# When the second-to-last batch's outputs are taken: behind its value product, between the last score units

## The chip, the cores and the metric

One core of one Trainium2 chip runs the whole kernel. TensorE (PE in the profile, PEld for its weight loads), VectorE (DVE), ScalarE (ACT) and GpSimd (POOL) each run their own list of instructions in order and wait for one another by semaphores; SyncE (SP) issues most of the DMAs. The metric is the device time of one execution in microseconds. A change within 0.2% (1.6 us here) counts as no change.

## The reference, cut to what matters

Input is x of 16 batches x 256 rows x 256 columns, float32. Two layers, each `x = x + s * silu(ffn(xn))` with `xn = layernorm(x)`. In the first layer `s` is a diagonal linear recurrence; in the second, the one that this change touches, it is an attention with 16 heads and a compressed key and value:

```python
q = (x @ Wq).reshape(B, S, 16, 192)              # 128 plain, 64 rotated
kv = x @ Wkv_a                                   # 64 latent columns, 64 rotated keys
c_kv = rmsnorm(kv[..., :64]) * kv_norm_w
k_nope, v = split(c_kv @ Wkv_b)                  # 16 heads x (128 + 128)
scores = einsum('bqhd,bkhd->bhqk', q, k) / sqrt(192)
attn = softmax(where(causal, scores, min))
out = einsum('bhqk,bkhd->bqhd', attn, v).reshape(B, S, 2048) @ Wo
x = x + out * silu(ffn2(xn))                     # ffn2: base + gated low-rank experts
```

The kernel folds `Wkv_b`'s key half into the queries and its value half into `Wo`. So the attention works on the 64 latent columns: scores are query x (latent, rotated key), the value product gives 64 latent columns per head, and one product with a folded matrix (`woe`, 1024 x 256) gives the output.

## The kernel before, in words

The second layer runs batch by batch (16 batches, numbered 0 to 15) in one long software pipeline. A step `n` of the loop is one unit of scores, 10 units per batch, and every engine's program is the same loop over `n` with its own work for each step. The names in this document:

- `scores n` (`l1_s`, L773 for units of the kinds W and M, L766 for kind T): TensorE's product for unit n into one of two banks. It waits (`mx`) until VectorE has read the unit two before it.
- `read n` (`most`, L1608, with L1600 for kind T): VectorE adds the mask, takes the row minimum and writes the tile to SBUF.
- `exps n` (L1065, ScalarE), `inverse n` (L1615, VectorE), `normalise n` (L2051, GpSimd), `turn n` (`turn_weights`, L1631 and L1644, VectorE: the weights transposed into `PT`). On every engine read n stands in step n, exps n in step n+1, inverse and normalise n in step n+2, turn n in step n+4.
- `value product` (`l1_pv`, L795, TensorE), which needs the turned weights of its batch. Batch 14 takes it in one piece. Batch 15 takes it in two: the first piece (key blocks for the first 6 units, 150 to 155) and the last piece, which needs turn 159 and, since it writes into the same banks, the low parts of the first piece's query tile (`otl`).
- `latents` (L1078, ScalarE) copies the value product of one query tile (two instructions, 128x512 each) out of PSUM as the high parts `oh`; `low parts` (L1653, VectorE, two instructions) writes the rest, `ol`. There is one pair `oh`/`ol` for each of the two query tiles.
- `output` (`l1_out`, L549, TensorE): 8 blocks x 3 matmuls (high x low, low x high, high x high, helper `three`) of 128x256. Then `gated_out` (L1664, VectorE) multiplies with the gate, `residual` (L2113, GpSimd) adds x, and SyncE stores 128 rows of the result.

I write output 14a, 14b, 15a, 15b for the two query tiles of the last two batches, and likewise for latents and low parts. The last batch (units 150 to 159) takes its units in an order of its own: M, M, M, T, T, M, and then four of kind W.

What sets the order around the change is a table written out by hand. For batches 0 to 13 a fixed lag behind the batch's last unit says at which step its value product (V), latents and low parts (L), outputs (O), gated outputs (R) and residuals (C) come. For batches 14 and 15 the table `LAST` names the step directly, one pair of numbers (query tile a, tile b) per batch. `due(what, n, qt)` looks the step up, and all engines' loops and the list that deals out the six PSUM banks shared by these products (`shared_bank_order`) use it. Within one step the order on each engine is fixed: on TensorE value product, scores, output; on ScalarE latents, then exps n-1; on VectorE low parts, gated_out, inverse n-2, turn n-4, read n.

Of the kernel before, what the change touches and what calls it, by code (L numbers as in the profile page):

```python
# [141 lines left out]
def shared_bank_order():  # L142
# [34 lines left out]

LAST = {
    "V": ((154, 154), (160, 162)),
    "L": ((158, 159), (163, 166)),  # L180
    "O": ((159, 161), (165, 167)),
    "R": ((161, 165), (166, 171)),
    "C": ((164, 165), (168, 173)),
}
LAG = {"V": (LAG_V, LAG_V), "L": (LAG_L, LAG_L), "O": LAG_O, "R": LAG_R, "C": LAG_C}
STEPS = max(LAST["C"][1]) + 1
# [2071 lines left out]
```

How the kernel before makes its waits and increments, by code:

```python
    def wait_ge(self, name, value):  # L99
        if value > self.reached.get(name, 0):
            self.e.wait_ge(self.sems[name], value)
            self.reached[name] = value
# [287 lines left out]
        def after_weights(w):  # L390
            w.wait_ge("wo_t", 4)
            w.wait_ge("wml", 1)
            w.wait_ge("wmh", 1)
# [1 line left out]
        def after_first(w):  # L395
            w.wait_ge("wo_t", 2)
# [1 line left out]
        def after_up(w):  # L398
            w.wait_ge("f1", 8 * NC)
# [1 line left out]
        def after_mlp(w):  # L401
            w.wait_ge("f1", 8 * NC)
            w.wait_ge("f2", 16 * NC)
            w.wait_ge("hsl", 8 * NC)
            w.wait_ge("hsh", 8 * NC)
            w.wait_ge("bu", NC)
# [1 line left out]
        def after_l0(w):  # L408
            after_mlp(w)
            w.wait_ge("xo", 2 * NC)
            w.wait_ge("th0", 2 * NC)
            w.wait_ge("dx", 2 * NC)
            w.wait_ge("ty", 2)
# [1 line left out]
        def qt_free(w, n):  # L415
            if n == 0:
                after_up(w)
            elif n < 3:
                after_mlp(w)
            else:
                w.wait_ge("s", UNITS * ((n - 3) // 2) + HALF_DONE[(n - 3) % 2])
# [10 lines left out]
        def place(e, w, b, h, heads=range(4)):  # L433
            n = 2 * b + h
            w.wait_ge("qq", g_nth[2 * n + 1])
            qt_free(w, n)
            for i in heads:
                for j in range(2):
# [7 lines left out]
        @block.sync  # L447
# [26 lines left out]
                load_x(c)  # L474
            w.wait_ge("w1h", 4)
            w.wait_ge("w1l", 4)
# [22 lines left out]
            def spread(b):  # L500
                w.wait_ge("kvw", b + 1)
                if b == 0:
                    after_mlp(w)
```

## Time and profile before

| what | value |
|---|---|
| median of 3 runs | 791.5 us (791.44 to 791.93) |
| the profiled execution, its own time | 791.67 us |
| its span, first to last instruction | 789.9 us |
| PE, DVE, ACT, POOL busy | 778.6, 681.7, 524.5, 479.5 us |
| mean granted TensorE clock | 0.999 |

The profiled execution is 0.17 us over the median, and 1.8 us of its time lie around the span. TensorE counts as busy 99% of the span, since each matmul's record overlaps the next one's. Only in the last 30 us are there stretches in which it waits.

### The profile page before, as it was taken

What the parts mean: (1) busy time and instruction counts of PE and PEld (TensorE: products, weight loads), DVE (VectorE), ACT (ScalarE), POOL (GpSimd) and SP (SyncE); (2) the same over time, 40 slices, a digit from 0 to 9 for tenths busy, and PEclk for the clock granted to TensorE, in tenths of its full rate; (3) what the DMA queues carried; (4) which work ended last, traced back from release to release, by engine and by line L of the source; (5) the groups of instructions that cost most, each with busy time, mean ns of one, the idle gap of its engine ahead of it and who ended that gap; (6) DMA issues with size and microseconds to landing.
All of it is one profiled execution on the core that took longest, in us unless ns stands there. A gap on an engine that the chain in (4) does not pass through costs nothing.

```text
span 789.9 us, 23152 instructions
## 1 busy us (share of the span) xinstructions
PE 778.6 (99%) x7976; PEld 711.5 (90%) x7976; DVE 681.7 (86%) x2616; ACT 524.5 (66%) x1612; POOL 479.5 (61%) x1278
## 2 busy tenths in 40 slices
PE   9999999999999999999999999999999999999988
PEld 7889889888889889898998989899898998989867
DVE  6998897888688899989898998989989898998885
ACT  5554454445555787777767777677777867777682
POOL 6880202202236696776867768686776867768673
PEclk9999999999999999999999999999999999999999
DMA  8600220000002222322222322223222222322220
GB/s 302 253 2 2 62 82 27 1 1 1 1 15 52 40 46 52 61 54 36 48 46 50 64 39 50 40 46 55 56 55 35 48 46 49 63 39 53 34 52 28
DMA packets 101334, 41.15 MB, mean 52 GB/s; under 512 B 91744, under 2 KB 98400, under 8 KB 100576
## 3 DMA queue, kind: packets, MB, share of 16 engines
q1 hardware_dynamic: 98896, 38.89, 22.1%
q8 instruction: 63, 1.03, 0.5%
q10 hardware_dynamic: 2320, 0.79, 0.4%
q14 instruction: 55, 0.45, 0.2%
HBM read 14.47 MB, written 4.19 MB: 24 GB/s over the span
## 4 chain that ended last, share of the span: by engine, by line
PE 92%; DVE 4%; ACT 1%; POOL 1%; issue 1%; ACTq 0%; POOLq 0%; DVEq 0%
PE bank L549 63%; PE bank L773 11%; PE bank L795 8%; PE bank L766 3%; PE bank L629 2%; PE bank L815 1%; PE bank L566 1%; DVE SM L1608 1%; PE bank L681 1%; ACT SM L1065 1%; DVE PT L1631 1%; PE bank L641 1%; PE bank L655 1%; POOL SM L2051 1%; PE bank L700 0%
## 5 line engine op out<-in xcount | busy, mean ns | idle before, releaser
L1065 ACT ACTIVATE SM<-SM,stb 128x224 f32<-128x224 f32 (+7 forms) x512 | 207.2, 407 | 62.7 <-DVE stb L1608 58.2
L2051 POOL TENSOR_SCALAR SM<-SM,stb 128x224 f32<-128x224 f32 (+7 forms) x512 | 195.2, 396 | 67.5 <-DVE stb L1615 66.1
L549 PE MATMUL bank<-yh,wq_lo 128*128 128x256 f32 x512 | 150.6, 294 | 0.0
L549 PE MATMUL bank<-yh,wq_hi 128*128 128x256 f32 x512 | 144.7, 283 | 0.0
L549 PE MATMUL bank<-yl,wq_hi 128*128 128x256 f32 x512 | 144.6, 282 | 0.0
L773 PE MATMUL bank<-KT,QT 128*128 128x192 f32 (+4 forms) x640 | 120.9, 327 | 1.7 <-DVE stb L1608 1.7
L1608 DVE CUSTOM_DVE_ANT_0 SM<-bank,CONST 128x224 f32<-128x224 f32 (+3 forms) x320 | 97.2, 348 | 23.3 <-PE bank L773 20.9
L1631 DVE STREAM_TRANSPOSE PT<-SM 128x128 f32<-128x128 f32 (+2 forms) x232 | 99.7, 462 | 16.7 <-PE bank L795 16.7
L773 PEld LDWEIGHTS bank<-KT,QT 128*128 128x128 f32 x640 | 97.5, 190 | 5.3 <-DVE stb L1608 3.6
L549 PEld LDWEIGHTS bank<-yh,wq_lo 128*128 128x128 f32 x512 | 97.1, 190 | 1.4
L549 PEld LDWEIGHTS bank<-yh,wq_hi 128*128 128x128 f32 x512 | 97.1, 190 | 0.0
L549 PEld LDWEIGHTS bank<-yl,wq_hi 128*128 128x128 f32 x512 | 97.0, 189 | 0.0
L1065 ACT ACTIVATION_READ_ACCUMULATOR SM<-SM,stb 128x1 f32 x512 | 96.9, 189 | 0.0
L950 ACT ACTIVATE hs<-bank,B 128x512 f32<-128x512 f32 x64 | 44.0, 688 | 75.3 <-PE bank L549 70.2
L2044 POOL TENSOR_TENSOR QA<-QA 128x256 f32<-128x256 f32 x62 | 45.9, 740 | 58.7 <-DVE QA L1579 58.7
L1037 ACT ACTIVATE QT<-bank 64x512 f32<-64x512 f32 x128 | 75.6, 590 | 6.5 <-PE bank L549 5.0
L1579 DVE TENSOR_TENSOR QA<-bank,TR 128x512 f32<-128x512 f32 x124 | 79.4, 683 | 0.1
L549 PE MATMUL bank<-woe_hi,ol 128*128 128x256 f32 x256 | 75.4, 294 | 0.7 <-issue 0.7
L549 PE MATMUL bank<-w2h,hl 128*128 128x256 f32 x256 | 74.0, 289 | 0.2 <-DVE w2l L1352 0.2
L549 PE MATMUL bank<-w2h,hh 128*128 128x256 f32 x256 | 72.4, 283 | 0.0
L549 PE MATMUL bank<-w2l,hh 128*128 128x256 f32 x256 | 72.3, 283 | 0.0
L549 PE MATMUL bank<-woe_hi,oh 128*128 128x256 f32 x256 | 72.1, 281 | 0.0
(229 smaller groups left out, 2068.9 us busy)
## 6 DMA issues: line engine op xcount, KB each, us to landing
QT<-QA SPq DMA_DIRECT2D x240, 64.0 KB, 2.1
PT<-KV SPq DMA_DIRECT2D x256, 16.0 KB, 1.8
out<-fo SPq DMA_DIRECT2D x32, 128.0 KB, 2.0
X<-in_x SPq DMA_DIRECT2D x7, 512.0 KB, 11.5
stage<-in_wqn SPq DMA_DIRECT2D x2, 1024.0 KB, 5.3
stage<-in_wo SPq DMA_DIRECT2D x2, 1024.0 KB, 4.9
stage<-in_w1t SPq DMA_DIRECT2D x4, 256.0 KB, 5.0
stage<-in_w2t SPq DMA_DIRECT2D x2, 512.0 KB, 6.2
```

Source lines behind the costliest of these rows:

```text
L549: i = e.matmul(dst, a, b, start=(first and j == 0), stop=(last and j == 2), skip_group_check=skip)
L766: j = e.matmul(sbank[n % 2][32 * i:32 * i + 32, at:to], KT[b % 3][:, p, 32 * kb:32 * kb + 32], Q[:, :, kb:3, i, :], start=True, stop=True)
L773: j = e.matmul(sbank[n % 2][:, at], Q[:, q, :, :].rearrange("p h c -> p (h c)"), KT[b % 3][:, p, 0:32 * q + 32], start=True, stop=True)
L795: j = e.matmul(sums[64 * half:64 * half + 64, :, 32 * q:32 * end], C[rows_, kb // 2, at], PT[rows_, 2 * half:2 * half + 2, kb, q:end, :], ...
L950: e.activation(hs[g % 2][:, :], fbank[g % 2][:, :], ACT.Gelu, bias=B1[:, g % 8:g % 8 + 1]).then_inc(SEM["gelu"], 1)
L1037: i = e.activation(QT[r, (2 * b + g // 2) % 3, p, :, g % 2:4:2, :].rearrange("p n j c -> p j n c"), src[r, :, :, :], ACT.Copy)
L1065: i = e.activation(M[:, at], M[:, at], ACT.Exp, bias=S[:, 0, j:j + 1], scale=-1.0, accum_out=S[:, 1, j:j + 1])
L1579: i = e.tensor_tensor(A[:, part, :, :, g % 2, :], src, TR[:, part, :].rearrange("p (n c) -> p n c", n=8).unsqueeze(1).broadcast_to([128, 2 ...
L1608: i = e.tensor_tensor_reduce(M[:, at], bk[:, at], mask[:, 224 - 32 * q:256], 1.0, 3e38, ALU.add, ALU.min, S[:, 0, j:j + 1])
L1631: return e.transpose(PT[:, slot, 0:k, q:q + some, :].rearrange("p k q c -> p q k c"), src)
L2044: e.tensor_tensor(A[:, 0, 0, :, :], A[:, 0, 0, :, :], A[:, 1, 1, :, :], ALU.subtract)
L2051: i = e.tensor_scalar(P[:, at], P[:, at], S[:, 2, j:j + 1], 1.0, ALU.mult, ALU.mult)
```

## The change

Five rows of the table `LAST` are there; four of them change. Batch 14's latents, low parts, outputs, gated outputs and residuals move to other steps, and batch 15's first latents and low parts move from step 163 to step 164. No instruction is added or removed, none changes its form.

```diff
 LAST = {
     "V": ((154, 154), (160, 162)),
-    "L": ((158, 159), (163, 166)),
-    "O": ((159, 161), (165, 167)),
-    "R": ((161, 165), (166, 171)),
-    "C": ((164, 165), (168, 173)),
+    "L": ((155, 157), (164, 166)),
+    "O": ((156, 158), (165, 167)),
+    "R": ((160, 165), (166, 171)),
+    "C": ((163, 166), (168, 173)),
 }
```

On TensorE, from scores 155 (three matmuls) on. A group of L549 is one output of 24 matmuls; here only its first row stands. The first L773 pair is scores 156. Before:

```order
L773 MATMUL bank<-KT0,QT 128x224 [waits mx]
L773 MATMUL bank<-KT0,QT 128x256
...
L549 MATMUL bank<-woe_hi,ol0 128x256 [waits z1,otl,oth]
...
L795 MATMUL bank<-PT 64x2x192 [waits otl,oth,c1,pt]
...
L549 MATMUL bank<-woe_hi,ol1 128x256 [waits ob]
...
L795 MATMUL bank<-PT 64x2x64 [waits otl,pt]
```

And now:

```order
L773 MATMUL bank<-KT0,QT 128x224 [waits mx]
L773 MATMUL bank<-KT0,QT 128x256
L549 MATMUL bank<-woe_hi,ol0 128x256 [waits z1,otl,oth]
...
L549 MATMUL bank<-woe_hi,ol1 128x256 [waits otl,oth]
...
L773 MATMUL bank<-KT0,QT 128x224 [waits mx]
L773 MATMUL bank<-KT0,QT 128x256
L795 MATMUL bank<-PT 64x2x192 [waits c1,pt]
...
L795 MATMUL bank<-PT 64x2x64 [waits otl,pt]
```

Before, scores 156 to 159 stood together, output 14a behind them and output 14b between the two pieces of batch 15's value product. Now output 14a stands behind scores 156, output 14b behind scores 158, and nothing is left between scores 159, the first piece and the last piece.

On VectorE, the end of its list, from read 159's last instruction on. L1653 is low parts 15a, the last L1631 of each piece is turn 159, L1664 is the gated output. Before:

```order
L1615 RECIPROCAL stb2<-stb2 128x2 [waits p]
L1631 STREAM_TRANSPOSE PT<-SM1 128x2x8x32 [waits n]
L1664 SCALAR_TENSOR_TENSOR fo0<-bank,PT 128x256 [waits out0,o]
L1615 RECIPROCAL stb3<-stb3 128x2 [waits p]
L1631 STREAM_TRANSPOSE PT<-SM2 128x2x8x32 [waits n]
L1631 STREAM_TRANSPOSE PT<-SM3 128x2x8x32 [waits n]
L1653 TENSOR_TENSOR ol0<-bank,oh0 128x512 [waits oth,pv]
L1653 TENSOR_TENSOR ol0<-bank,oh0 128x512 [waits oth]
L1631 STREAM_TRANSPOSE PT<-SM4 128x2x8x32 [waits n]
```

And now:

```order
L1664 SCALAR_TENSOR_TENSOR fo0<-bank,PT 128x256 [waits out0,o]
L1615 RECIPROCAL stb2<-stb2 128x2 [waits p]
L1631 STREAM_TRANSPOSE PT<-SM1 128x2x8x32 [waits n]
L1615 RECIPROCAL stb3<-stb3 128x2 [waits p]
L1631 STREAM_TRANSPOSE PT<-SM2 128x2x8x32 [waits n]
L1631 STREAM_TRANSPOSE PT<-SM3 128x2x8x32 [waits n]
L1631 STREAM_TRANSPOSE PT<-SM4 128x2x8x32 [waits n]
L1653 TENSOR_TENSOR ol0<-bank,oh0 128x512 [waits oth,pv]
L1653 TENSOR_TENSOR ol0<-bank,oh0 128x512 [waits oth]
```

Low parts 15a and turn 159 have changed places, and gated output 14a stands one step earlier. Earlier in the same list low parts 14a now stand ahead of inverse 153 (before: of inverse 156), and low parts 14b ahead of inverse 155 (before: of inverse 157). On ScalarE latents 14a now stand between exps 153 and exps 154, latents 14b between exps 155 and exps 156. GpSimd's and SyncE's lists are the same as before. In the deal of the banks, output 15a now takes the bank of output 14a and output 15b that of output 14b.

## Rows read from the trace of the kernel before

**Rows 1.** Chain of waits in order of time: start us, length us, what
```profile
748.46 0.81 PE bank L773 x4
...
772.14 0.77 DVE PT L1631 x2
...
772.96 2.60 PE bank L795 x92
775.56 3.04 PE bank L549 x24
...
780.52 3.05 PE bank L549 x24
```

**Rows 2.** Timeline of TensorE: start, length, instruction, idle before
```profile
748.29 0.97 PE L773 MATMUL bank<-KT,QT 128*128 128x224 f32 x4
...
758.44 4.22 PE L795 MATMUL bank<-PT 32*64 32x512 f32 x128
...
765.13 1.08 PE L773 MATMUL bank<-KT,QT 128*128 128x224 f32 x4 [0.65 <-DVE stb L1608]
...
769.76 0.36 PE L549 MATMUL bank<-woe_hi,ol 128*128 128x256 f32 x1 [0.71 <-issue]
...
772.56 0.28 PE L549 MATMUL bank<-woe_hi,oh 128*128 128x256 f32 x1
...
778.53 1.99 PE L795 MATMUL bank<-PT 32*64 32x128 f32 x128
```

**Rows 3.** Timeline of VectorE, same columns
```profile
749.30 0.39 DVE L1608 CUSTOM_DVE_ANT_0 SM<-bank,CONST 128x224 f32<-128x224 f32 x1 [0.24 <-PE bank L773]
...
763.57 0.14 DVE L1615 RECIPROCAL stb<-stb 128x6 f32<-128x6 f32 x1
...
765.13 0.19 DVE L1615 RECIPROCAL stb<-stb 128x6 f32<-128x6 f32 x1
...
768.37 1.29 DVE L1653 TENSOR_TENSOR ol<-bank,oh 128x512 fp32r<-128x512 f32 x2 [0.46 <-ACT oh L1078]
769.57 0.16 DVE L1615 RECIPROCAL stb<-stb 128x2 f32<-128x2 f32 x1
...
770.87 1.29 DVE L1653 TENSOR_TENSOR ol<-bank,oh 128x512 fp32r<-128x512 f32 x2
...
772.82 0.36 DVE L1608 CUSTOM_DVE_ANT_0 SM<-bank,CONST 128x224 f32<-128x224 f32 x1
...
774.68 0.17 DVE L1615 RECIPROCAL stb<-stb 128x2 f32<-128x2 f32 x1
774.76 1.28 DVE L1631 STREAM_TRANSPOSE PT<-SM 128x512 f32<-128x512 f32 x2
776.31 1.29 DVE L1653 TENSOR_TENSOR ol<-bank,oh 128x512 fp32r<-128x512 f32 x2 [0.27 <-ACT oh L1078]
777.52 0.70 DVE L1631 STREAM_TRANSPOSE PT<-SM 128x512 f32<-128x512 f32 x1
```

**Rows 4.** Timeline of ScalarE, same columns
```profile
762.99 0.32 ACT L1065 ACTIVATE SM<-SM,stb 128x32 f32<-128x32 f32 x1 [0.38 <-DVE stb L1608]
...
765.11 0.41 ACT L1065 ACTIVATE SM<-SM,stb 128x128 f32<-128x128 f32 x1
...
766.27 0.19 ACT L1065 ACTIVATION_READ_ACCUMULATOR SM<-SM,stb 128x1 f32 x1
...
767.74 1.09 ACT L1078 ACTIVATE oh<-bank 128x512 fp32r<-128x512 f32 x2
...
775.61 1.09 ACT L1078 ACTIVATE oh<-bank 128x512 fp32r<-128x512 f32 x2 [0.96 <-PE bank L795]
```

**Rows 5.** Timeline of GpSimd: normalise 159
```profile
774.94 0.91 POOL L2051 TENSOR_SCALAR SM<-SM,stb 128x224 f32<-128x224 f32 x2 [0.32 <-DVE stb L1615]
```

**Rows 6.** Busy times by stretch; behind POOL the granted clock, DMA share
```profile
786.00:787.00 1.00, 0.41 (x4) 0.20 (x2) 0.42 (x1) 0.00 (x0) 0.05 (x1) 1.00 0.11 35
...
788.50:789.00 0.50, 0.00 (x0) 0.00 (x0) 0.00 (x0) 0.00 (x0) 0.00 (x0) 0.94 0.77 260
```

## The prediction

> **What bounds the kernel now.** The edit touches only the last 30 us, so I went first to the chain of waits there, in order of time, then to the timelines of the engines it passes through. In the chain [rows 1] VectorE's turn 155 ends at 772.91, and it releases the first piece of batch 15's value product at 772.96. From there TensorE never waits: first piece 2.60, output 14b 3.04, last piece (starts 778.53 [rows 2]), output 15a 3.05, output 15b. So two things set the end: when VectorE has done its list up to turn 155, and how much TensorE work stands behind that point.
>
> Before 772.96 TensorE does wait. In its timeline [rows 2] scores 157 start at 765.13 after 0.65 us of waiting for read 155, and output 14a starts at 769.76 after 0.71 us. VectorE is the engine that nearly all of this waits for: in its timeline [rows 3] the marked gaps are 0.46 at 768.37 (low parts 14a, waiting for ScalarE's latents) and 0.27 at 776.31. The change moves an output of 24 matmuls from behind 772.96 to before it. The question is whether TensorE's own sum was the bound behind 772.96, or only just covered something else.
>
> **The change, step by step.** I replay the stretch with the durations of before. TensorE's value product of batch 14 starts at 758.44 and lasts 4.22 [rows 2]. All up to there is untouched.
>
> Latents 14a. ScalarE took latents 15a 0.05 behind the value product (first piece 772.96 + 2.60 [rows 1], latents 775.61 [rows 4]), so latents 14a start at 762.71. They last 1.09 and now stand ahead of exps 154, which started at 762.99 and now start at 763.80: 0.81 later. Inverse 154, which came 2.14 behind that start (765.13 [rows 3]), can go from 765.94. VectorE is itself later than that by now, so this costs nothing.
>
> Low parts 14a. On VectorE they now stand ahead of inverse 153 (763.57 [rows 3]). Their first input is ready at 762.71 + 0.63 (latents 767.74 [rows 4] to low parts 768.37 [rows 3]) = 763.34. The pair takes 1.20 to the next instruction (768.37 to 769.57 [rows 3]). So all that follows is 1.20 later: read 155 ends and exps 155 start at 765.11 + 1.20 = 766.31.
>
> Output 14a. It can start 1.39 behind its low parts (768.37 to 769.76 [rows 2, 3]): 764.96, and takes 2.92 (24 matmuls, the last starts at 772.56 [rows 2], 0.12 apart). TensorE is free at 767.88, then takes scores 157 and 158 at 0.81 each (the chain's row of 748.46 [rows 1]): 769.50. Scores 157 are up to 2.75 later than before, but VectorE comes to read them only some 0.7 behind 769.5 (below), so it does not notice.
>
> Latents and low parts 14b. ScalarE does exps 155 from 766.31 for 1.35 (765.11 to 766.27 + 0.19 [rows 4]), then latents 14b at 767.68, low parts 14b at 768.31. That is where low parts 14a were before (768.37), and VectorE again waits for ScalarE there, some 0.6 us: the 0.46 of before, one unit less in front of it (1.30, from 769.57 to 770.87 [rows 3]), one pair of low parts more (1.20), rounded. VectorE goes on at 769.51.
>
> Output 14b. 768.31 + 1.39 = 769.70, done at 772.62. It stands ahead of scores 159. So scores 159 start at 772.62, and VectorE can read them 1.01 later (748.29 [rows 2] to 749.30 [rows 3]): 773.63, not 772.82 as before. VectorE would be there at 769.51 + 2 units at 1.30 + 0.75 (turn 155, from 770.87 + 1.20 to 772.82) = 772.86, and waits 0.77. This wait is new.
>
> First piece. Turn 155 is done in time, so it starts behind scores 159 at 772.62 + 0.81 = 773.43: 0.47 later than before. It ends at 776.03.
>
> The tail. Before, inverse 159 came 1.86 behind the start of read 159 (772.82 to 774.68 [rows 3]); now 773.63 + 1.86 = 775.49. The gated output 14a, moved ahead of it, lies in the wait for exps 159 as it did before. Then turns 157, 158, 159 at 0.64 each (two took 1.28 [rows 3]) from 775.57: turn 159 ends at 777.49. GpSimd's normalise 159 is done 1.17 behind inverse 159 (774.94 + 0.91 [rows 5], against 774.68), at 776.66, in time for turn 159 at 776.85. Latents 15a start at 776.08 and give their first half at 776.71, also in time. Low parts 15a start at 777.50, and the last piece, which needs them, 1.39 later: 778.89. Before it started at 778.53 [rows 2]. Behind it nothing changes: the last piece, outputs 15a and 15b, gate, residual, store.
>
> So output 14b's 3.04 us do leave the tail, and in their place TensorE waits 776.03 to 778.89 = 2.86 us, for a chain on VectorE that output 14b had hidden. The sum is +0.36 us.
>
> Things that I cost at nothing: the bank deal (output 15a now waits for gated output 14a, done by 774.7; output 15b for gated output 14b, which VectorE does behind low parts 15a, near 779.1, over four us before it is wanted); the residuals and stores of batch 14, which GpSimd and SyncE do while idle. If gated output 14b were late by its own length of about 0.4 nothing would follow.
>
> **Bounds.** From below: suppose VectorE waits nowhere from 763.57 on. It was done with turn 159 at 777.52 + 0.62 = 778.14 with low parts 15a in front of it [rows 3], the same work as now, and had waited 0.46 + 0.27 + some 0.2 of small gaps. So it could be done at 777.2 and the last piece start at 777.4: -1.1 us. From above: each step that I hid may cost its own size. The two waits on VectorE (0.6 and 0.77) could each grow by half a microsecond, giving about +1.4. I take the replay, +0.36.
>
> The profiled execution took 791.67 us, so the sum is 792.03; it lies 0.17 over the median of 791.5, so the forecast is 791.9 as a median.
>
> **Rivals.** A, the forecast: TensorE's saved cover comes back as a wait, 791.9, within about 790.9 to 793.0.
>
> B, better packing: the two VectorE waits shrink since latents 14b or scores 159 come earlier than I have them. For it: TensorE's own waits before 772.96 add up to over 1.3 us in two rows alone [rows 2], and the freed output fills them. Against it: the order on each engine is fixed, and both waits follow from an instruction that stands in front (exps 155, output 14b). At its bound it is -1.1 us, about 790.4; its middle is 791.0. It cannot reach 789.9, which is 0.2% under the median, so it too is mostly "no change". 0.2% is 1.6 us, about what can be told from no change here.
>
> C, slower: the clock falls in the new gap. At the very end of the trace TensorE's last matmul ends at 786.41 and the granted clock, 1.00 at first, averages 0.94 from 788.50 to 789.00 [rows 6]: it fell from 2.4 to 1.2 GHz at about 788.94, some 2.5 us after the last matmul. The new wait of 2.86 us is longer than that. For it: that row. Against it: no inner wait of this trace is near this length, none shows a fall, and one fall in one execution does not say that each such wait brings one. If the clock falls before 778.89, the 48 matmuls of the last two outputs, 0.12 apart, run at the lower level for as long as it lasts. If all of them take twice their time that is +5.7 us, with the last piece's 1.99 up to +7.7; if it is up again after one output, +2.9. No row shows how soon it rises. I take +2.9 on top of the 0.36: 794.8. It decides from a wait of 2.5 us up; with a VectorE chain 0.4 shorter it is gone.
>
> The Trainium skill, TensorE: Matmul & The Clock Gate, section Part 1: The HAM clock gate, says that the clock is at half rate by default, that activity releases it, and that the check runs on its own time, not the kernel's. By that rule this stretch would come out slower in some executions and not in others. The trace agrees as far as the fall at 788.94 goes; the recovery no row here shows. From the same page (Back-to-back issue gap), 256 columns take 213 ns cold; by that the 48 matmuls would cost an estimated +4.5 us if all ran cold, not +5.7.
>
> D, the change does nothing: were the last piece bound by something that did not move, the time would be 791.5. Nothing in the trace has that place; the number is inside A.
>
> **Chances.** A (with D) 0.72, B 0.13, C 0.15. Slower by over 0.2% (above 793.1): nearly all of C and a little of A, 0.15. Faster by over 0.2%: 0.04, since B's bound stops short of it. Same: 0.81. The forecast is A's, 791.9. The range reaches down to B's bound, 790.5, and up through A's +1.4 into C's mild cases, 793.8; about 0.1 is left out above and little below.
>
> **What the profile will show.** Right: outputs 14a and 14b on TensorE near 765.0 and 769.7; VectorE idle for about 0.8 us before read 159, released by TensorE's scores 159; the chain of waits going through VectorE's turns and low parts 15a into the last piece, with TensorE idle from 776.0 to 778.9; the granted clock at 1.00 throughout. Wrong: a first piece that starts before 773.0 or after 774.2; output 14b waiting past 770.5; low parts 15a waiting for ScalarE rather than for turn 159; a clock under 1.00 between 776 and 786, which would be C. A time under 789.9 would break the bound on VectorE's work, and so the whole replay.

## The result, and the profile after

The changed kernel takes 793.21 us (median of 22 executions, 791.53 to 794.35), the kernel before 791.53 us (median of 22, 791.34 to 792.82). The means have a ratio of 1.0016, with a 95% interval of 1.0010 to 1.0023; the medians are 1.68 us or 0.21% apart. So the change is slower, but the interval reaches to both sides of the 0.2% that I had named as the limit, and whether it is slower by more than that stays open. The time lies in my range (790.5 to 793.8), but 1.3 us above the forecast, and the likeliest case was not the one that happened. Rival C was.

The profiled execution took 793.82 us, its span is 792.0 us, against 791.67 and 789.9. The chain of waits of after, in order of time, has these pieces at its end (start us, length us, what):

```profile
765.35 3.09 PE bank L549 x24
768.43 1.62 PE bank L773 x8
770.05 3.07 PE bank L549 x24
773.12 0.82 PE bank L773 x4
...
776.01 1.16 DVE PT L1631 x2
...
777.73 1.26 DVE ol L1653 x2
...
779.12 2.51 PE bank L795 x118
781.63 4.07 PE bank L549 x24
```

The order is the one foreseen. Output 14a (765.35), scores 157 and 158, output 14b (770.05), scores 159 stand in a row. Then the chain leaves TensorE for VectorE's turns and low parts 15a (777.73) and comes back with the last piece. Of before's chain [rows 1], output 14b (775.56) is gone from between the pieces. What is new are two lengths: the last piece takes 2.51 instead of 1.99 [rows 2], output 15a 4.07 instead of 3.05.

TensorE's timeline of after around that place (start, length, instruction, idle before):

```profile
758.87 4.21 PE L795 MATMUL bank<-PT 32*64 32x512 f32 x128
```

```profile
779.12 2.51 PE L795 MATMUL bank<-PT 32*64 32x128 f32 x128 [2.66 <-DVE ol L1653]
781.56 0.58 PE L549 MATMUL bank<-woe_hi,ol 128*128 128x256 f32 x1
...
783.01 0.41 PE L549 MATMUL bank<-woe_hi,ol 128*128 128x256 f32 x1
783.22 0.41 PE L549 MATMUL bank<-woe_lo,oh 128*128 128x256 f32 x1
...
784.32 0.28 PE L549 MATMUL bank<-woe_hi,oh 128*128 128x256 f32 x1
784.44 0.28 PE L549 MATMUL bank<-woe_hi,ol 128*128 128x256 f32 x1
```

The same place in the trace of before, where output 15a starts at full speed:

```profile
780.45 0.39 PE L549 MATMUL bank<-woe_hi,ol 128*128 128x256 f32 x1
```

And the stretches of after (from:to, its length, busy time and instructions of PE, PEld, DVE, ACT, POOL; then the granted clock, DMA share, GB/s):

```profile
776.00:778.00 2.00, 0.46 (x40) 0.32 (x21) 2.00 (x5) 1.09 (x2) 1.71 (x4) 1.00 0.03 8
778.00:779.00 1.00, 0.00 (x0) 0.00 (x0) 1.00 (x3) 0.00 (x0) 0.00 (x0) 1.00 0.38 129
779.00:780.00 1.00, 0.88 (x61) 0.91 (x66) 0.30 (x1) 0.00 (x0) 0.61 (x1) 1.00 0.01 2
780.00:781.00 1.00, 1.00 (x71) 1.00 (x63) 0.00 (x0) 0.00 (x0) 0.11 (x1) 0.70 0.02 7
781.00:782.00 1.00, 1.00 (x32) 0.88 (x19) 0.00 (x0) 0.33 (x1) 0.00 (x0) 0.50 0.42 140
782.00:783.00 1.00, 1.00 (x6) 1.00 (x6) 0.63 (x2) 0.76 (x2) 0.00 (x0) 0.50 0.00 0
783.00:784.00 1.00, 1.00 (x7) 1.00 (x7) 0.66 (x2) 0.00 (x0) 0.00 (x0) 0.60 0.00 0
784.00:785.00 1.00, 1.00 (x11) 1.00 (x10) 0.00 (x0) 0.00 (x0) 0.00 (x0) 1.00 0.00 0
```

TensorE waits 2.66 us ahead of the last piece, for low parts 15a. At about 780.4 the granted clock falls from 2.4 to 1.2 GHz (its mean is 0.70 from 780 to 781, 0.50 from there) and is back at about 783.8 (0.60 from 783 to 784). In between output 15a's matmuls start 0.21 apart, afterwards 0.12, as everywhere before. TensorE works all through the low stretch: it waits first, and pays later.

The difference of the two profiled executions, 2.1 us of span, comes out in three parts:

- 0.43 us stand there before the instructions of the two kernels differ: batch 14's value product starts at 758.87, not at 758.44 [rows 2].
- From that start to the last piece it is 779.12 - 758.87 = 20.25 us, before 778.53 - 758.44 = 20.09 [rows 2]. The new order costs 0.16.
- From the last piece's start to output 15b it is 781.63 + 4.07 - 779.12 = 6.58 us, before 780.52 + 3.05 - 778.53 = 5.04 [rows 1, 2]. The low clock costs 1.54.

0.16 + 1.54 = 1.70, and the medians are 1.68 apart. That these agree so closely is in part chance, since executions differ by more than that, but the clock splits them: 16 of the 22 have a mean granted clock of 0.997 or 0.998 and took 793.12 us or more (793.56 on average), the other 6 have 1.0 and took 791.53 to 792.70 (792.18 on average).

The 0.43 us arise long before the first instruction that differs. From one value product near 290 us to the next near 325 it is 33.93 us in before (290.64 to 324.57) and 34.74 in after (290.27 to 325.01), so a lead of 0.37 turns into a lag of 0.44. In between TensorE waits 0.58 us, at 306.73, for a product of VectorE (L1579) that had itself waited for a DMA; the trace of before has neither wait. VectorE's timeline of after:

```profile
305.30 1.29 DVE L1579 TENSOR_TENSOR QA<-bank,TR 128x512 f32<-128x512 f32 x2 [1.88 <-DMA QT<-QA]
```

### The profile page after: what moved, and what is told of

It is laid out like the page before. It is cut to its first block, busy times and chain, and to the rows that moved or that the text cites. A ratio compares the mean times of both kernels' runs of the same rounds, so it can differ in the third digit from the quotient of the medians.

```text
span 792.0 us, 23152 instructions
## 1 busy us (share of the span) xinstructions
PE 779.1 (98%) x7976; PEld 712.3 (90%) x7976; DVE 681.2 (86%) x2616; ACT 522.7 (66%) x1612; POOL 480.3 (61%) x1278
## 4 chain that ended last, share of the span: by engine, by line
PE 90%; SPq 4%; DVE 2%; issue 1%; DMA 1%; ACT 1%; POOL 0%; POOLq 0%; DVEq 0%
PE bank L549 63%; PE bank L773 12%; PE bank L795 8%; SPq L512 3%; PE bank L766 2%; PE bank L629 2%; SPq L441 1%; PE bank L566 1%; PE bank L681 1%; PE bank L641 1%; PE bank L655 1%; DMA QT<-QA 0%; PE bank L700 0%; ACT SM L1065 0%; PE bank L706 0%
## 5 line engine op out<-in xcount | busy, mean ns | idle before, releaser
L549 PE MATMUL bank<-yh,wq_lo 128*128 128x256 f32 x512 | 150.5, 294 | 0.0
L549 PE MATMUL bank<-yh,wq_hi 128*128 128x256 f32 x512 | 144.6, 282 | 0.0
L549 PE MATMUL bank<-yl,wq_hi 128*128 128x256 f32 x512 | 144.6, 282 | 0.0
L773 PE MATMUL bank<-KT,QT 128*128 128x192 f32 (+4 forms) x640 | 120.4, 327 | 0.4 <-DVE stb L1608 0.4
L1631 DVE STREAM_TRANSPOSE PT<-SM 128x128 f32<-128x128 f32 (+2 forms) x232 | 99.3, 459 | 16.0 <-PE bank L795 16.0
L773 PEld LDWEIGHTS bank<-KT,QT 128*128 128x128 f32 x640 | 97.6, 190 | 2.8 <-DVE stb L1608 1.1
L549 PEld LDWEIGHTS bank<-yh,wq_lo 128*128 128x128 f32 x512 | 97.1, 190 | 1.4
L549 PEld LDWEIGHTS bank<-yh,wq_hi 128*128 128x128 f32 x512 | 97.0, 190 | 0.0
L549 PEld LDWEIGHTS bank<-yl,wq_hi 128*128 128x128 f32 x512 | 97.0, 189 | 0.0
L1579 DVE TENSOR_TENSOR QA<-bank,TR 128x512 f32<-128x512 f32 x124 | 79.3, 682 | 2.0 <-DMA QT<-QA 1.9
L549 PE MATMUL bank<-woe_hi,ol 128*128 128x256 f32 x256 | 75.9, 297 | 0.4 <-issue 0.4
L549 PE MATMUL bank<-w2h,hl 128*128 128x256 f32 x256 | 74.0, 289 | 0.2 <-DVE w2l L1352 0.2
L549 PE MATMUL bank<-woe_hi,oh 128*128 128x256 f32 x256 | 72.5, 283 | 0.0
L549 PE MATMUL bank<-w2h,hh 128*128 128x256 f32 x256 | 72.4, 283 | 0.0
L549 PE MATMUL bank<-woe_lo,oh 128*128 128x256 f32 x256 | 72.4, 283 | 0.0
```

The source lines that it names most:

```text
L549: i = e.matmul(dst, a, b, start=(first and j == 0), stop=(last and j == 2), skip_group_check=skip)
L773: j = e.matmul(sbank[n % 2][:, at], Q[:, q, :, :].rearrange("p h c -> p (h c)"), KT[b % 3][:, p, 0:32 * q + 32], start=True, stop=True)
L1579: i = e.tensor_tensor(A[:, part, :, :, g % 2, :], src, TR[:, part, :].rearrange("p (n c) -> p n c", n=8).unsqueeze(1).broadcast_to([128, 2 ...
L1631: return e.transpose(PT[:, slot, 0:k, q:q + some, :].rearrange("p k q c -> p q k c"), src)
```

## The experiments

All runs were timed in five rounds against the kernel before on the same chip. Experiments 1, 2 and 5 ran on one chip, 3, 4 and 6 on a second, 7 on a third. "Fell" below means a mean granted clock of 0.998 or less over the whole execution; where in the execution the clock fell, only a trace can show. The kernel before fell in 0 of 33, 1 of 27 and 1 of 21 executions on the three chips, 2 of 81 in all.

**1. The changed kernel again.** No edit.

> The changed kernel once more, on the same chip as the three others, to have its distance to them from one chip. Theory C: most executions carry a granted clock below 1.0 and lie 1.5 us or so above the few at 1.0; median 793.2, the ones at 1.0 near 791.9 (or, with the second level that before also shows, 792.5). Rival (order alone): the time does not go with the clock.

793.17 us; 8 of 11 fell, these took 793.06 to 793.48 us, the three others 791.61, 791.98 and 792.57. The time goes with the clock, as expected. The profile happened to catch one that did not fall:

```profile
758.61 4.22 PE L795 MATMUL bank<-PT 32*64 32x512 f32 x128
...
778.85 1.98 PE L795 MATMUL bank<-PT 32*64 32x128 f32 x128 [2.66 <-DVE ol L1653]
```

Same order, same 2.66 us of waiting, last piece 20.24 us behind the value product's start, but 1.98 long and with the outputs behind it at full speed: own time 791.98. This is the execution that the replay had described.

**2. The wait filled, in two sizes.** 16 or 6 matmuls that nobody reads, behind the first piece:

```diff
+                if n == 160:
+                    w.wait_ge("mx", TOTAL - 1)
+                    for i in range(16):      # 6 in the second kernel
+                        e.matmul(sbank[0][:, 0:256], woe_hi[:, i % 8, 0:128], woe_hi[:, i % 8, :], start=True, stop=True)
```

> The changed kernel, with 16 extra 128x256 matmuls on TensorE right behind the first piece of batch 15's value product, in the wait ahead of the last piece. They write a bank that nobody reads. At 0.12 us each they fill 1.9 of the 2.66 us that the trace of after shows there. Theory C (the wait lets the clock fall from 2.4 to 1.2 GHz, and that costs 1.5 to 1.7 us): no fall ahead of the last piece, granted clock at its upper level through the last two outputs, time about 791.9, that is 1.2 to 1.7 below the change. Rival (the +1.7 us is the order itself, VectorE's chain and the wait): the wait for VectorE is as long as before, so the time stays at 793.2.

> As the run with 16 extra matmuls, but only 6 of them (0.7 us), so that a wait of about 1.9 us is left. Theory C with a fall that depends on the length of the wait: fewer executions with a clock under its upper level than with none added, so a median between 791.9 and 793.2, nearer to 791.9. If the fall needs only any wait near 2 us, it stays at 793.2. Rival (order alone): 793.2.

With 16: 791.63 us, ratio to before 1.0005 (0.9996 to 1.0014), 0 of 11 fell. With 6: 791.65 us, ratio 1.0007 (0.9999 to 1.0016), 3 of 11 fell (793.04, 793.18, 794.13 us). TensorE's timelines, first with 16, then with 6 (L902 is the extra work, and the four added lines turn L1653 into L1657):

```profile
758.18 4.22 PE L795 MATMUL bank<-PT 32*64 32x512 f32 x128
...
775.71 2.18 PE L902 MATMUL bank<-woe_hi 128*128 128x256 f32 x16
778.44 1.98 PE L795 MATMUL bank<-PT 32*64 32x128 f32 x128 [0.55 <-DVE ol L1657]
```

```profile
758.10 4.22 PE L795 MATMUL bank<-PT 32*64 32x512 f32 x128
...
775.61 0.98 PE L902 MATMUL bank<-woe_hi 128*128 128x256 f32 x6
778.34 1.98 PE L795 MATMUL bank<-PT 32*64 32x128 f32 x128 [1.75 <-DVE ol L1657]
```

The last piece starts 20.26 and 20.24 us behind the value product, as late as without the extra work. So adding 16 matmuls makes the changed kernel 1.5 us faster, level with before but no better, and the order's own cost of 0.1 to 0.2 stays. The rival that put the whole loss on the order and VectorE's chain is out. With 6 the median came out lower than I had expected, since only 3 of 11 executions fell.

**3. The same wait in the old order.** One number in the table of before:

```diff
-    "O": ((159, 161), (165, 167)),
+    "O": ((159, 162), (165, 167)),
```

> The kernel before with one number changed: output 14b at step 162 instead of 161, so it stands behind the last piece of batch 15's value product instead of between the two pieces. Everything else, the scores, latents and low parts, is as before. TensorE then waits between the pieces for VectorE's turn 159 (done at 778.1 in before, first piece done at 775.6): about 2.6 us, in the order of before. The output's 3.04 us now come behind the last piece, which starts at most 0.35 earlier, so 2.7 are added in any case: 794.2. Theory C (the wait alone brings the fall, whatever the order around it): in half or more of the executions the clock falls there and 1.5 more are added, 795.7, granted clock 0.997 or 0.998; median over 795. Rival (the fall belongs to the new order of outputs and scores): 794.2 with the clock at 0.999 or 1.0 throughout.

795.84 us (5 executions), ratio 1.0053 (1.0040 to 1.0065), all 5 fell. TensorE's timeline and its stretches:

```profile
758.51 4.21 PE L795 MATMUL bank<-PT 32*64 32x512 f32 x128
...
778.34 3.20 PE L795 MATMUL bank<-PT 32*64 32x128 f32 x128 [2.71 <-DVE PT L1631]
```

```profile
778.00:779.00 1.00, 0.66 (x40) 0.67 (x48) 0.28 (x1) 0.00 (x0) 0.00 (x0) 0.87 0.00 0
779.00:780.00 1.00, 1.00 (x52) 1.00 (x48) 0.00 (x0) 0.00 (x0) 0.00 (x0) 0.50 0.00 0
...
781.00:782.00 1.00, 1.00 (x34) 0.88 (x19) 0.00 (x0) 0.00 (x0) 0.00 (x0) 0.50 0.05 16
782.00:783.00 1.00, 1.00 (x10) 1.00 (x9) 0.00 (x0) 0.00 (x0) 0.00 (x0) 0.92 0.00 0
```

The clock falls here too, near 778.7, with nothing moved but output 14b. The last piece starts 19.83 us behind the value product, the 0.26 earlier that the missing output allowed, and lasts 3.20. The kernel is 4.2 us slower than before on this chip: output 14b's 3.04 us now come behind the last piece, less the 0.26, and the last piece is 1.21 us longer than the 1.99 of before. That makes 4.0, and the two outputs behind it take 6.21 where two of before take 6.10, which adds 0.1. The fall belongs to the wait, not to the new order.

**4. The last turn ahead of the last low parts, undone.**

```diff
-    "L": ((155, 157), (164, 166)),
+    "L": ((155, 157), (163, 166)),
```

> The changed kernel with one part undone: latents and low parts 15a at step 163 again, so turn 159 stands behind low parts 15a on VectorE, as before. Low parts 15a then wait a little for ScalarE's latents, turn 159 follows them, and the last piece starts behind that, by my reckoning 0.1 us earlier than in the changed kernel. The wait of TensorE stays at about 2.5 us. Theory C: the clock falls as in the changed kernel, 793.1. Rival (the exchange of these two is what costs): 791.5.

793.11 us, ratio to before 1.0012 (1.0003 to 1.0020); 6 of 11 fell. The ones that did not took 791.69 to 792.24. TensorE's timeline, and one of its stretches (PE's busy time alone):

```profile
758.97 4.21 PE L795 MATMUL bank<-PT 32*64 32x512 f32 x128
...
779.29 3.46 PE L795 MATMUL bank<-PT 32*64 32x128 f32 x128 [2.71 <-DVE PT L1631]
```

```profile
779.00:780.00 1.00, 0.71 (x27) 0.58 0.09 28
```

The last piece starts 20.32 us behind the value product, against 20.25 in the change. So the exchange gains 0.07 in these two traces; I had reckoned that it costs 0.1. The rival, that the exchange is what makes the change slow, is out. The clock falls here at about 779.2, shortly before the last piece begins, and all of that piece runs at the low level: 3.46 us.

**5. Output 14a alone moved early.**

```diff
-    "L": ((158, 159), (163, 166)),
-    "O": ((159, 161), (165, 167)),
+    "L": ((155, 159), (163, 166)),
+    "O": ((156, 161), (165, 167)),
```

> One part of the change alone: latents and low parts 14a at step 155 and output 14a at step 156 (its bank order with it); 14b, 15a and the gated outputs stay as before, so output 14b still stands between the two pieces of the value product. By my replay VectorE no longer waits 0.46 us for latents 14a, turn 155 ends up to 0.4 us earlier, and output 14b still covers VectorE's chain: TensorE waits nowhere behind the first piece, the clock stays up. Theory C and the replay: 791.1 to 791.4, 0.1 to 0.4 below before. Rival (moving output 14a itself costs, by delaying scores 157): 791.9 or more.

792.54 us, ratio 1.0013 (1.0004 to 1.0022); 5 of 11 fell, these took 793.16 to 793.99, the others 791.76 to 792.54. My replay was wrong here, twice. TensorE's timeline, then VectorE's:

```profile
758.26 4.22 PE L795 MATMUL bank<-PT 32*64 32x512 f32 x128
...
773.10 2.61 PE L795 MATMUL bank<-PT 32*64 32x384 f32 x96 [2.56 <-DVE PT L1631]
```

```profile
768.66 0.39 DVE L1608 CUSTOM_DVE_ANT_0 SM<-bank,CONST 128x224 f32<-128x224 f32 x1 [0.41 <-PE bank L773]
...
771.02 1.29 DVE L1653 TENSOR_TENSOR ol<-bank,oh 128x512 fp32r<-128x512 f32 x2 [0.31 <-ACT oh L1078]
```

VectorE waits 0.41 for scores 157, which stand behind output 14a and are now missed, since low parts 14b no longer fill that time; the wait for latents, which was to vanish, is 0.31 ahead of low parts 14b, so the two are more than the 0.46 of before. The last piece comes at 778.68, 20.42 us behind the value product. And TensorE does wait: 2.56 us, now ahead of the first piece. The long wait had only changed its place, and the kernel fell again, though not in the execution that was profiled.

**6. Low parts 14b behind the first piece.** TensorE's order as before:

```diff
-    "L": ((158, 159), (163, 166)),
+    "L": ((157, 160), (163, 166)),      # (158, 160) in the second kernel
```

> Away from both kernels: TensorE's order exactly as before, but latents and low parts 14a one step earlier (157) and 14b one step later (160), so that one pair of low parts (1.2 us) leaves VectorE's list ahead of turn 155. Output 14a can then start right behind scores 159, near 769, and the first piece behind it, near 772 instead of 772.96. Output 14b still stands between the pieces and covers VectorE's chain. Last piece at 777.7 to 778.2 instead of 778.53: 790.7 to 791.2, wait between the pieces under 0.3 us, clock up. Rival (ScalarE's latents 14b now stand ahead of exps 159 and delay inverse 159 by 0.6): last piece no earlier, 791.5 or more.

> As the kernel with 14a at 157 and 14b at 160, but latents and low parts 14a stay at step 158 as before; only 14b moves by one step. Output 14a then starts where it did (769.76) and ends at 772.68, and turn 155 is done before that, so the first piece starts 0.28 earlier than before and the last piece 0.25: 791.2. If it comes out like the version with 157, the early latents 14a are worth nothing. Rival (ScalarE's latents 14b delay inverse 159): 791.5 or more.

793.55 us (1.0020, 1.0012 to 1.0029; 6 of 11 fell) and 792.64 us (1.0012, 1.0003 to 1.0021; 0 of 11). Both expectations failed. TensorE's timelines, first with 14a at 157, then with 158:

```profile
769.61 1.08 PE L773 MATMUL bank<-KT,QT 128*128 128x224 f32 x4 [2.03 <-DVE stb L1608]
...
773.92 2.60 PE L795 MATMUL bank<-PT 32*64 32x384 f32 x96 [0.38 <-DVE ol L1653]
```

```profile
758.36 4.21 PE L795 MATMUL bank<-PT 32*64 32x512 f32 x128
...
773.92 2.60 PE L795 MATMUL bank<-PT 32*64 32x384 f32 x96 [1.17 <-DVE ol L1653]
```

The releaser of the first piece is L1653: it waits for low parts 14b, not for turn 155. The first piece writes into the banks of batch 14's value product, so they must have been read out before. In the first kernel it starts 15.63 us behind the value product (758.29), in the second 15.56, not 14.52 as before [rows 1, 2], and all of the tail follows. That 1.04 us is the whole loss of the second kernel, whose clock stays up: its median is 1.01 us over that of before.

**7. Early latents without a long wait.** Two last tables, the first with before's order on TensorE, the second with output 14a behind scores 157:

```diff
-    "L": ((158, 159), (163, 166)),
-    "O": ((159, 161), (165, 167)),
+    "L": ((155, 159), (163, 166)),      # second kernel: (155, 157)
+    "O": ((159, 161), (165, 167)),      # second kernel: (157, 161)
```

> TensorE's order exactly as before, 14b as before; only latents and low parts 14a come at step 155 as in the change. ScalarE's latents then lie ahead of exps 154, and VectorE takes low parts 14a without waiting (0.46 us of waiting gone). Low parts 14b stay ahead of the first piece, which the two runs with 14b at 160 showed to be needed: its banks are theirs. TensorE's longest wait stays near 1.2 us, so by theory C no fall. First piece 0.1 to 0.4 earlier than before, time 791.1 to 791.4, level with before or just under it. Rival (scores 157 to 159, each up to 1.2 us later now, leave VectorE waiting): 791.6 or more.

> The change's early latents and low parts (14a at 155, 14b at 157), but with the outputs where they leave no long wait: output 14a behind scores 157 (step 157), output 14b between the two pieces as before; the rest as before. By my replay scores 158 and 159 are there before VectorE asks for them, and TensorE waits some 1.1 us ahead of the first piece, nowhere over 1.9. Theory C: no fall or few; time 791.2 to 791.5. Rival (any early low parts cost, as in the change, whatever stands in the tail): 791.7 or more, or a clock at 0.998 in many executions.

791.56 us (ratio 1.0000, 0.9991 to 1.0009; 2 of 11 fell) and 791.54 us (0.9997, 0.9988 to 1.0006; 0 of 11). TensorE's timeline of the first, then of the second:

```profile
758.25 4.22 PE L795 MATMUL bank<-PT 32*64 32x512 f32 x128
...
766.14 1.08 PE L773 MATMUL bank<-KT,QT 128*128 128x224 f32 x4 [1.84 <-DVE stb L1608]
...
778.42 1.99 PE L795 MATMUL bank<-PT 32*64 32x128 f32 x128
```

```profile
758.31 4.22 PE L795 MATMUL bank<-PT 32*64 32x512 f32 x128
...
766.19 1.08 PE L773 MATMUL bank<-KT,QT 128*128 128x224 f32 x4 [1.84 <-DVE stb L1608]
...
772.73 2.60 PE L795 MATMUL bank<-PT 32*64 32x384 f32 x96 [0.97 <-DVE PT L1631]
...
778.30 1.99 PE L795 MATMUL bank<-PT 32*64 32x128 f32 x128
```

In the second the last piece starts 19.99 us behind the value product, 0.10 earlier than before, and its waits (1.84, 0.97) stay short, with output 14a behind the longer one. It is level with before: better by the trace's 0.1, but the interval holds 1, so a gain is not shown. In the first I had put the longest wait at 1.2; it is 1.84. I had also expected a first piece 0.1 to 0.4 earlier, and it comes 14.55 us behind the value product, not 14.52: early latents alone gain nothing.

Falls by TensorE's longest wait from 755 us to the last output, in the profiled execution of each kernel. Only the traces of the change and of experiments 3 and 4 caught a fall; that the falls of the other kernels stand behind their longest wait is inferred from the mean clock, not seen.

| kernel | longest wait, us | fell |
|---|---|---|
| 16 matmuls filled in | 0.55 | 0 of 11 |
| before | 0.71 | 2 of 81 |
| 14b at 160, 14a at 158 | 1.17 | 0 of 11 |
| 6 matmuls filled in | 1.75 | 3 of 11 |
| early latents, outputs as before | 1.84 | 2 of 11 |
| early latents, output 14a behind scores 157 | 1.84 | 0 of 11 |
| 14b at 160, 14a at 157 | 2.03 | 6 of 11 |
| 14a alone early | 2.56 | 5 of 11 |
| the change (both series) | 2.66 | 24 of 33 |
| change with 15a at step 163 | 2.71 | 6 of 11 |
| before with output 14b last | 2.71 | 5 of 5 |

## Why the prediction was right and where it was wrong

**The replay of the order was right.** The run of the kernel again (experiment 1, value product at 758.61, 0.17 later than before) has output 14a at 765.08 (foreseen 764.96) and the last piece at 778.85 (778.89). Taken from the value product's start, the last piece is 0.15 later than before where I had said 0.36. The missing 0.21 comes from two places. About half is there by output 14b, which starts 11.16 behind the value product in after and 11.26 by my numbers; the rest is in the three turns ahead of low parts 15a, 1.81 from the first (775.92) to low parts 15a (777.73) where I had 1.93. The new wait of VectorE ahead of read 159 was foreseen as 0.77 and is 0.73, TensorE's wait was foreseen as 2.86 and is 2.66. VectorE's timeline of after:

```profile
768.60 1.29 DVE L1653 TENSOR_TENSOR ol<-bank,oh 128x512 fp32r<-128x512 f32 x2 [0.51 <-ACT oh L1078]
...
773.97 0.39 DVE L1608 CUSTOM_DVE_ANT_0 SM<-bank,CONST 128x224 f32<-128x224 f32 x1 [0.73 <-PE bank L773]
...
777.73 1.25 DVE L1653 TENSOR_TENSOR ol<-bank,oh 128x512 fp32r<-128x512 f32 x2
```

**The step that failed is the chance of C.** I had the wait, its length, the row that showed a fall 2.5 us after the last matmul, and the form of the cost. I then argued that one fall in one execution says little, and that no inner wait of this trace showed one. That second point was no evidence: before's longest inner wait is 0.71 in this stretch and 1.17 in the whole trace, so the trace had no wait that could have shown it. The new wait was longer than the one after which a fall was seen, and 0.15 was far too little for that: 24 of 33 executions fell. The condition that I gave with it, that C decides from 2.5 us up and is gone with a chain 0.4 shorter, does not hold either: the kernels with a longest wait of 2.03 and 1.75 fell in 6 and 3 of 11. And I had the fall within the wait, where only experiment 4 shows it; in after it came 1.3 us behind the wait's end.

**The price of C was too high.** I took 2.9 of a possible 7.7 for want of a row that shows the clock coming back. In the profiled execution it came back at 783.8, and the low stretch (780.4 to 783.8) cost 1.54: 0.52 in the last piece (781.56 - 779.12 = 2.44 against 780.45 - 778.53 = 1.92, the start of output 15a in both timelines) and 1.02 in output 15a. Output 15b ran at full speed. In experiment 3 the low clock cost 1.3 (1.21 in the last piece, 0.11 behind it), in experiment 4 1.5, nearly all in the last piece. Had I given C its chance and its size, the forecast would have been 791.5 + 0.16 + 1.54 = 793.2. That the measured time lies in the range is partly luck: by my own price C stood at 794.8, outside it, and the time came in because the clock came back sooner than I had priced.

**The Trainium skill's rule.** The Trainium skill (TensorE: Matmul & The Clock Gate, Part 1: The HAM clock gate) has the check behind the clock run on its own time, not from the kernel's start. The runs agree with that: the same kernel with the same wait fell in 24 executions and did not in 9; that this is the reason, no run here shows. By the Trainium skill's formula for the low clock (same page, Back-to-back issue gap), 256 columns take an estimated 213 ns. The trace agrees: 0.21 between the starts at 783.01 and 783.22.

**B and D.** B did not happen: no version's last piece came more than 0.26 us earlier than before, inside the bound of 1.1, and that one only by pushing an output behind it. The bound itself was too kind, since it did not count that the first piece also waits for low parts 14b (experiment 6). D is out: the last piece starts 0.16 later, and the low clock costs 1.54.

**Left open.** Both kernels have executions over a microsecond above their lowest with the clock up (before 791.41 to 792.82 on the third chip, the change 791.53 to 792.70). The late DMA near 306 us that makes the profiled execution of after 0.43 us late is one source; the traces of experiments 1 and 4 have it too, with waits of TensorE of 0.22 and 0.51 us there. Why it is late in some executions, and whether it makes up the whole spread, is not shown. What besides the wait decides whether an execution falls is open as well. And length alone does not set the number of falls: two kernels with the same 1.84 us have 2 and 0 of 11, and eleven executions each do not tell these apart.

## What to carry to other kernels

An output that seems to sit in the way of TensorE's tail may be the work that covers another engine's chain there; moving it forward turns its time into a wait, and the sum over TensorE does not show it. Price a wait of TensorE twice: its length, and the clock it may cost afterwards, here 1.3 to 1.5 us, in some half or more of the executions of the kernels with a wait of 2 us or more. Where such a wait cannot be avoided and dense work stands behind it, work for TensorE in the wait, even work that nobody needs, took the falls away here; it brought the kernel back to before, not below it. Look at the granted clock of each execution, not only at the median.

## What the runs showed of the hardware that was not expected

A kernel whose longest wait is 1.75 us already fell in 3 of 11 executions, the one with 2.66 us in 24 of 33. The fall has no fixed place: it came 3.9 us after the first piece's end in after (776.46 to 780.4, when TensorE had been at work again for 1.3 us), 3.1 us in experiment 3 (775.63 to 778.7), and 2.6 us in experiment 4 (776.58 to 779.2, still inside the wait). Small matmuls pay as well: the last piece, 128 matmuls of 32x64 operands, lasts 1.98 us on the high clock and 3.46 in experiment 4, where all of it runs on the low one.
